# A state scan's C products: every C row spread to SBUF by DMA, VectorE multiplying pairs of states

## The chip, the cores and the metric

One core of a Trainium2 chip runs the whole program. The metric is device time in microseconds (us) of one execution, the median of several.

## What is computed

Four layers work one after the other on an image tensor x of shape (2, 96, 48, 48). The change touches one stage of the first layer, the selective scan of a 2D state space block: E = 192 channels, N = 16 states, K = 4 scan directions, L = 2304 positions. In the notation of the kernel, for each channel, direction and state n, along the positions i:

```
h[n, i] = exp(-A[n] * dlt[i]) * h[n, i-1] + B[n, i] * v'[n, i]
y[i]    = sum over n of C[n, i] * h[n, i]        (+ Ds * x, further down)
```

B and C belong to an image and a state, not to a channel, so each of their rows is needed on all the partitions (channels) of its image. The four directions' y are added up. The other layers and stages are the same in both kernels.

## The kernel before

Two images of 192 channels make T = 3 tiles of 128 partitions. A tile's scan over one direction is cut into NSEG = 3 segments of SEG = 768 positions. One (tile, direction, segment) is a **unit** u; there are U = 36, each with N = 16 states, so J = 576 **steps** j. All of it is in `l0_scan`, with the order of every engine written out by hand and counted semaphores between them. For step j:

- SyncE (`loads`, lines 696 to 700) brings a unit's dlt, na, B rows (Bp), v and C rows (Cp). B and C rows lie there in bf16 in three parts that sum to f32.
- TensorE spreads the B row of state n over the 128 partitions into PSUM: `b_rows`, two matmuls by a selecting matrix (line 729).
- ScalarE writes r = tanh(...) (line 889) and the decay exp(-A dlt) into PSUM (line 879, in two parts).
- VectorE makes r = (r + 1) * B, `b_r` (line 804, four steps ahead: AHEAD = 4).
- GpSimd multiplies two states of r by v, `times_v` (line 842, 1536 elements per partition). All of GpSimd's operands are in SBUF.
- VectorE runs the recurrence, `tensor_tensor_scan` (line 830), with the decay from PSUM and r from SBUF, into h.
- C times h is made in one of two ways. `BY_VECTOR` lists the states that VectorE multiplies: five in sixteen on average, 180 of the 576, one at a time (`times_c`, line 811), with C spread by TensorE into PSUM (`c_rows`, again line 729, from Cp). The other 396 are multiplied by GpSimd in 198 pairs (`times_c`, line 851), with C in SBUF: a DMA per image half reads two C rows from DRAM and writes them to 64 partitions each (line 712, tile `cb`, NCB = 4 slots).
- TensorE adds C*h into y in PSUM by an identity matmul, `add_y` (line 762), LATE = 5 steps behind.
- Once per unit, after state 9, VectorE makes the running sum of dlt for the next unit (`cumsum`, line 794). Once per unit ScalarE takes y out of PSUM (lines 872, 875).

What sets the order around the change: on VectorE a step is b_r(j+4), then times_c(j-1) where that state is VectorE's, then the scan of j. On GpSimd a pair of steps is times_v(j), then a pair of C products. PSUM holds one B row and one C row at a time, so a B row waits until the last one is used, and b_r and `c_rows` wait for each other too.

Of the kernel before, what the change touches and what calls it, by code (L numbers as in the profile page):

```python
# [592 lines left out]
def l0_scan(nc, a, ps, ident, Y, d):  # L593
# [5 lines left out]

    with ExitStack() as ctx:
        sb, sem = space(nc, ctx, "l0c")
        NR, NHV, NHP, NCB = 8, 3, 4, 4
        AHEAD, LATE, LAG = 4, 5, 6
        BY_VECTOR = ((2, 5, 10, 13), (2, 5, 8, 11, 12, 15))
        dlt, v, S = (sb(n, [128, 2, SEG]) for n in ("dlt", "v", "S"))
        Ds, dsum = sb("Ds", [128, T, K]), sb("dsum", [128, T])
        Bp, Cp = (sb(n, [3 * B * N, 2, SEG], BF16) for n in ("Bp", "Cp"))  # L610
# [13 lines left out]
        s_own, s_shared, s_tanh, s_w, s_b, s_c, s_S, s_init = map(  # L624
            sem, ("own", "shared", "tanh", "w", "b", "c", "S", "init"))
        PB, PC, PY = 0, SEG, 3 * BANK
# [5 lines left out]
        NLOAD = 5  # L632
# [4 lines left out]
        assert all(b == a + 1 and a // N == b // N for a, b in zip(others[::2], others[1::2]))  # L637

        def by_pool(j):
            return j not in with_c  # L640
# [4 lines left out]
        def pool_steps(j):  # L645
            return j - taken[j]
# [33 lines left out]

            return slice(BANK, SEG) if e % 2 == 0 else slice(0, MID)

        b_all, c_all, y_all = (ps[:, o:o + SEG] for o in (PB, PC, PY))
        da = [ps[:, o:o + SEG] for o in PDA]

        @block.sync
        def _(sp):
            def loads(u):
                t, k, c0 = place(u)
                i = u % 2  # L690
                if u >= 2:

                    sp.wait_ge(s_scan, (u - 1) * N + 1)
                if u % (K * NSEG) == 0:
                    sp.dma_start(sel[:, t % 2, :], a["sel"][t]).then_inc(s_sel[t % 2], 16)
                sp.dma_start(dlt[:, i, :], d["dlt"][t * K + k, :, c0:c0 + SEG]).then_inc(s_in[i], 16)
                sp.dma_start(na[:, i, :], d["na"][t * K + k]).then_inc(s_in[i], 16)
                sp.dma_start(Bp[:, i, :], d["bc"][k, 0, :, c0:c0 + SEG]).then_inc(s_in[i], 16)
                sp.dma_start(v[:, i, :], d["v"][t * K + k, :, c0:c0 + SEG]).then_inc(s_in[i], 16)
                sp.dma_start(Cp[:, i, :], d["bc"][k, 1, :, c0:c0 + SEG]).then_inc(s_in[i], 16)  # L700

            loads(0)
            sp.dma_start(Ds[:, :, :], a["Ds"]).then_inc(s_ds, 16)
            for j in range(J):
                u, n = divmod(j, N)
                if by_pool(j) and pool_steps(j) % 2 == 0:
                    t, k, c0 = place(u)
                    p = pool_steps(j)
                    if p >= NCB:
                        sp.wait_ge(s_hp, p - NCB + 2)  # L710
                    for i in range(2):
                        sp.dma_start(cb[64 * i:64 * i + 64, p % NCB:p % NCB + 2, :],
                                     d["cf"][k, 2 * t + i, n:n + 2, c0:c0 + SEG].unsqueeze(0)
                                     .to_broadcast([64, 2, SEG])).then_inc(s_cb[p % NCB // 2], 16)
                if n == (0 if u == 0 else 2) and u + 1 < U:
                    loads(u + 1)
            for i in range(2):
                sp.wait_ge(s_in[i], 16 * NLOAD * U // 2)
                sp.wait_ge(s_sel[i], 16 * ((T + 1 - i) // 2))
            for i in range(NCB // 2):  # L720
                sp.wait_ge(s_cb[i], 32 * len(range(2 * i, pool_steps(J), NCB)))

        @block.tensor
        def _(pe):
            def spread(rows, at, j, done):
                i, n = (j // N) % 2, j % N
                t = j // (N * NSEG * K)
                for lo, hi in pieces(at):
                    mm = pe.matmul(ps[:, lo:hi], sel[:, t % 2, n * 128:(n + 1) * 128], rows[:, i, lo - at:hi - at],  # L729
                                   start=True, stop=True)  # L730
                mm.then_inc(done, 1)

            def b_rows(j):
                u = j // N
                if j % N == 0:
                    pe.wait_ge(s_in[u % 2], (u // 2 + 1) * (16 * NLOAD))
                    t = u // (K * NSEG)
                    pe.wait_ge(s_sel[t % 2], 16 * (t // 2 + 1))
                if j:
                    pe.wait_ge(s_ub, j)  # L740
                if j - AHEAD - 1 > 0:
                    pe.wait_ge(s_hv, dve_steps(j - AHEAD - 1))
                spread(Bp, PB, j, s_b)

            def c_rows(j):
                if j:
                    pe.wait_ge(s_hv, dve_steps(j))
                pe.wait_ge(s_ub, min(j + AHEAD + 1, J))
                spread(Cp, PC, j, s_c)

            def add_y(j):
# [12 lines left out]
                mm.then_inc(s_y, 1)
                if place(u)[1] and 4 <= n < 4 + len(y_pieces(u)):
                    lo, hi, src = y_pieces(u)[n - 4]
                    pe.matmul(ps[:, lo:hi], ident[:, :], src, start=False, stop=False)

            for j in range(AHEAD + 1):
                b_rows(j)  # L770
            for j in range(J + LATE):
                if j < J and not by_pool(j):
                    c_rows(j)
                if j + AHEAD + 1 < J:
                    b_rows(j + AHEAD + 1)
                if j >= LATE:
                    add_y(j - LATE)

        @block.vector
        def _(dve):  # L780
# [36 lines left out]
            for j in range(J):  # L817
# [1702 lines left out]
```

## Time and profile before

| | |
|---|---|
| median of 3 runs | 2978.03 us |
| lowest, highest | 2972.81, 2978.46 us |
| the profiled execution: its own time | 2974.61 us |
| its span in the trace | 2972.7 us |
| its mean granted TensorE clock | 0.941 |

The profile is of one execution. Times are us unless marked ns; PE is TensorE, PEld its weight loads, DVE VectorE, ACT ScalarE, POOL GpSimd, SP SyncE. A row of the page names the line, the engine, the operation, what it writes and reads with shapes, the count, the busy time and mean length in ns, and the idle time before it with what ended that. The state scan runs from about 300 to 2001 us of the span.

### The profile page before, as it was taken

To read this page: it belongs to the slowest core of one execution; us is meant where nothing else is said; L and a number is where in the kernel's file an instruction comes from. 1 tells how busy PE (TensorE), PEld (TensorE's weight loads), DVE (VectorE), ACT (ScalarE), POOL (GpSimd) and SP (SyncE) were. 2 spreads that over 40 slices of the span, in tenths; PEclk is the share of its full clock that TensorE was granted. 3 is DMA by queue.
4 is the path that set the end of the run, shared out by engine and by line. 5 is a ranking of instruction groups with operands and counts; after the bars stand their busy time and mean duration, and the time that the engine had idled before them with its cause. 6 is when DMAs were issued, how large, how long until landed. Compare 5 with 4: busy or idle time off the path is not lost. (4 is left out here: it accounts for less than half of the span.)

```text
span 2972.7 us, 24549 instructions
## 1 busy us (share of the span) xinstructions
PE 2162.6 (73%) x7460; PEld 1057.5 (36%) x7460; DVE 2552.8 (86%) x2138; ACT 1575.5 (53%) x2301; POOL 1939.5 (65%) x645
## 2 busy tenths in 40 slices
PE   6853566676766666776666677678985999798579
PEld 3421223333332333333323333334432555354444
DVE  5678899999999999999999999986887777699620
ACT  1565677777777777777776777753230000362220
POOL 0165899999999999999999999984000000297000
PEclk9977799999999999999999999998897999899689
DMA  1276444444454444445444454535005443100360
GB/s 48 88 221 235 119 111 115 111 125 121 107 129 110 120 117 114 119 108 129 109 118 123 112 125 100 125 84 180 0 1 153 115 116 96 38 8 16 78 88 24
DMA packets 140258, 308.71 MB, mean 104 GB/s; under 512 B 47643, under 2 KB 63264, under 8 KB 135136
## 3 DMA queue, kind: packets, MB, share of 16 engines
q1 hardware_dynamic: 139040, 303.01, 40.3%
q10 hardware_dynamic: 1088, 4.13, 0.6%
q8 instruction: 62, 1.02, 0.2%
q14 instruction: 68, 0.56, 0.1%
HBM read 220.30 MB, written 46.87 MB: 90 GB/s over the span
## 5 line engine op out<-in xcount | busy, mean ns | idle before, releaser
L842 POOL TENSOR_TENSOR l0c_r<-l0c_r,l0c_v 128x1536 f32<-128x1536 f32 x288 | 990.6, 3447 | 51.1 <-DVE l0c_r L804 49.3
L879 ACT ACTIVATE ps<-l0c_dlt,l0c_na 128x512 f32<-128x512 f32 (+1 forms) x1152 | 626.1, 575 | 474.6 <-DVE l0c_h L830 460.1
L830 DVE TENSOR_TENSOR_SCAN l0c_h<-ps,l0c_h,l0c_r 128x768 f32<-128x768 f32 x384 | 693.3, 1806 | 1.2 <-issue 0.6
L851 POOL TENSOR_TENSOR l0c_hcp<-l0c_cb,l0c_h 128x1536 f32<-128x1536 f32 x198 | 682.9, 3449 | 1.4 <-issue 1.4
L762 PE MATMUL ps<-l0c_hcp,net_ident 128*128 128x512 f32 (+1 forms) x1584 | 586.6, 493 | 17.6 <-ACT l_Z L872 7.1
L889 ACT ACTIVATE l0c_r<-l0c_S,l0c_floor,l0c_na 128x768 f32<-128x768 f32 x576 | 580.1, 1014 | 18.0 <-issue 18.0
L729 PE MATMUL ps<-l0c_Bp,l0c_sel 96*128 96x512 bf16 (+1 forms) x1152 | 289.3, 333 | 379.5 <-DVE l0c_r L804 180.3
L804 DVE SCALAR_TENSOR_TENSOR l0c_r<-l0c_r,ps 128x768 f32<-128x768 f32 x576 | 533.1, 926 | 6.6 <-PE ps L729 3.9
L762 PEld LDWEIGHTS ps<-l0c_hcp,net_ident 128*128 128x128 f32 x1584 | 272.1, 192 | 268.7 <-issue 195.7
L830 DVE TENSOR_TENSOR_SCAN l0c_h<-ps,l0c_r 128x768 f32<-128x768 f32 x192 | 335.0, 1745 | 0.0
L1541 PE MATMUL ps<-l_prod,l_wa 128*96 128x384 f32 (+1 forms) x888 | 291.8, 492 | 25.8 <-DVE l_prod L1458 25.8
L729 PEld LDWEIGHTS ps<-l0c_Bp,l0c_sel 96*128 96x128 bf16 x1152 | 83.2, 97 | 571.5 <-DVE l0c_r L804 487.4
L762 PE MATMUL ps<-l0c_hcv,net_ident 128*128 128x512 f32 x720 | 266.0, 492 | 0.0
L167 POOL MEMSET l2g_pad<- 96x224 f32 (+1 forms) x8 | 1.8, 268 | 326.5 <-SPq L118 326.5
L1541 PEld LDWEIGHTS ps<-l_prod,l_wa 128*96 128x96 f32 (+1 forms) x888 | 146.3, 165 | 170.7 <-issue 161.6
L729 PE MATMUL ps<-l0c_Cp,l0c_sel 96*128 96x256 bf16 x360 | 88.9, 328 | 158.9 <-DVE l0c_r L804 138.4
L1678 PE MATMUL ps<-l_rows,l_diag 128*128 128x384 f32 x468 | 159.4, 503 | 16.1 <-DMA l_rows<-l2g_pad 11.3
L811 DVE TENSOR_TENSOR l0c_hcv<-ps,l0c_h 128x768 f32<-128x768 f32 x180 | 170.6, 948 | 0.1
L762 PEld LDWEIGHTS ps<-l0c_hcv,net_ident 128*128 128x128 f32 x720 | 123.9, 192 | 109.9 <-issue 88.9
L1607 POOL TENSOR_TENSOR l_accp<-l_accp,l_prod 128x1152 f32<-128x1152 f32 x54 | 142.3, 2636 | 29.2 <-ACT l_prod L1626 21.9
L1458 DVE TENSOR_TENSOR l_prod<-l_turned,l_other 128x2304 f32<-128x2304 f32 (+1 forms) x48 | 122.6, 2557 | 41.1 <-PE ps L1541 38.2
L1658 DVE SCALAR_TENSOR_TENSOR ps<-l_rows,net_kern,ps 128x1152 f32<-128x1152 f32 x105 | 149.4, 1423 | 3.7
(273 smaller groups left out, 2286.2 us busy)
## 6 DMA issues: line engine op xcount, KB each, us to landing
l0c_cb<-cf SPq DMA_DIRECT2D x396, 384.0 KB, 5.5
l_other<-l_p SPq DMA_DIRECT2D x22, 864.0 KB, 5.9
dlt<-l0s_dl SPq DMA_DIRECT2D x36, 384.0 KB, 2.3
v<-l0s_vv SPq DMA_DIRECT2D x36, 384.0 KB, 2.9
l0c_dlt<-dlt SPq DMA_DIRECT2D x36, 384.0 KB, 3.4
l0c_v<-v SPq DMA_DIRECT2D x36, 384.0 KB, 4.5
l_other<-l_p SPq DMA_DIRECT2D x22, 288.0 KB, 6.7
l0c_Bp<-bc SPq DMA_DIRECT2D x36, 144.0 KB, 3.7
```

The costliest lines, as they stand in the source:

```text
L729: mm = pe.matmul(ps[:, lo:hi], sel[:, t % 2, n * 128:(n + 1) * 128], rows[:, i, lo - at:hi - at], start=True, stop=True)
L762: mm = pe.matmul(ps[:, lo:hi], ident[:, :], hc[:, lo - PY:hi - PY], start=(n == 0), stop=(n == N - 1))
L804: dve.scalar_tensor_tensor(rj, rj, 1.0, b_all, ALU.add, ALU.mult).then_inc(s_ub, 1)
L811: dve.tensor_tensor(hcv[:, dve_steps(j) % NHV, :], c_all, h[:, j % N, :], ALU.mult).then_inc(s_hv, 1)
L830: dve.tensor_tensor_scan(h[:, n, :], da[j % 2], r[:, j % NR, :], init, ALU.mult, ALU.add).then_inc(s_scan, 1)
L842: pool.tensor_tensor(two, two, v[:, (j // N) % 2, :].unsqueeze(1).to_broadcast([128, 2, SEG]), ALU.mult).then_inc(s_w, 2)
L851: pool.tensor_tensor(hcp[:, p % NHP:p % NHP + 2, :], cb[:, p % NCB:p % NCB + 2, :], h[:, e % N:e % N + 2, :], ALU.mult).then_inc(s_hp, 2)
L879: act.activation(da[e % 2][:, part], dlt[:, i, part], ACT.Exp, scale=na[:, i, n:n + 1]).then_inc(done, 1)
L889: act.activation(r[:, j % NR, :], S[:, i, :], ACT.Tanh, bias=floor[:, :], scale=na[:, i, N + n:N + n + 1]).then_inc(s_tanh, 1)
L1541: mm = pe.matmul(ps[0:C, o:o + CH], wa[0:height, i, :], prod[0:height, n % NPR, c * CH:(c + 1) * CH], start=(i == 0), stop=(i == PT - 1))
L1658: ins = dve.scalar_tensor_tensor(sums, src, kern[:, tl, tap:tap + 1], sums, ALU.mult, ALU.add)
L1678: mm = pe.matmul(ps[:, o:o + CH], diag[:, tl, i, :], rows[:, tl, dy + 8 * c:dy + 8 * c + 8, dx:dx + W], start=(i == 0), stop=(i == NPE - 1))
```

## The change

- Every state's C rows come to SBUF by the spreading DMA, for VectorE's states too: 576 transfers in place of 396, into `cb` with NCB = 6 slots (three pairs). The slot is now given by the step's number j. SyncE waits for the engine that used the slot: GpSimd's or VectorE's count.
- `c_rows`, the tile Cp and its load, the PSUM area of C and the semaphore s_c are gone.
- VectorE's states are pairs now: (4, 5), (12, 13) in an even unit, (2, 3), (8, 9), (14, 15) in an odd one, 180 of 576 as before. `times_c` multiplies two states of h by two rows of cb in one instruction of 1536 elements, at the even step two steps later, with hcv at NHV = 4 slots.
- Waits that go: b_r's on s_c, and the B rows' on s_hv. `add_y` of a VectorE state waits until both of its pair are made.

```diff
-        NR, NHV, NHP, NCB = 8, 3, 4, 4
+        NR, NHV, NHP, NCB = 8, 4, 4, 6
-        BY_VECTOR = ((2, 5, 10, 13), (2, 5, 8, 11, 12, 15))
+        BY_VECTOR = ((4, 5, 12, 13), (2, 3, 8, 9, 14, 15))
...
-                sp.dma_start(Cp[:, i, :], d["bc"][k, 1, :, c0:c0 + SEG]).then_inc(s_in[i], 16)
...
-                if by_pool(j) and pool_steps(j) % 2 == 0:
+                if j % 2 == 0:
                     t, k, c0 = place(u)
-                    p = pool_steps(j)
-                    if p >= NCB:
-                        sp.wait_ge(s_hp, p - NCB + 2)
+                    if j >= NCB:
+
+                        if by_pool(j - NCB):
+                            sp.wait_ge(s_hp, pool_steps(j - NCB) + 2)
+                        else:
+                            sp.wait_ge(s_hv, dve_steps(j - NCB) + 2)
                     for i in range(2):
-                        sp.dma_start(cb[64 * i:64 * i + 64, p % NCB:p % NCB + 2, :],
+                        sp.dma_start(cb[64 * i:64 * i + 64, j % NCB:j % NCB + 2, :],
...
-                if j - AHEAD - 1 > 0:
-                    pe.wait_ge(s_hv, dve_steps(j - AHEAD - 1))
                 spread(Bp, PB, j, s_b)
-
-            def c_rows(j):
-                if j:
-                    pe.wait_ge(s_hv, dve_steps(j))
-                pe.wait_ge(s_ub, min(j + AHEAD + 1, J))
-                spread(Cp, PC, j, s_c)
...
-                    pe.wait_ge(s_hv, dve_steps(j) + 1)
+                    pe.wait_ge(s_hv, dve_steps(j) // 2 * 2 + 2)
...
-                if j > AHEAD:
-                    dve.wait_ge(s_c, dve_steps(j - AHEAD))
...
-            def times_c(j):
-                dve.wait_ge(s_scan, j + 1)
-                dve.wait_ge(s_c, dve_steps(j) + 1)
-                if dve_steps(j) >= NHV:
-                    dve.wait_ge(s_y, with_c[dve_steps(j) - NHV] + 1)
-                dve.tensor_tensor(hcv[:, dve_steps(j) % NHV, :], c_all, h[:, j % N, :], ALU.mult).then_inc(s_hv, 1)
+            def times_c(e):
+                q = dve_steps(e)
+                dve.wait_ge(s_scan, e + 2)
+                dve.wait_ge(s_cb[e % NCB // 2], 32 * (e // NCB + 1))
+                if q >= NHV:
+                    dve.wait_ge(s_y, with_c[q - NHV + 1] + 1)
+                dve.tensor_tensor(hcv[:, q % NHV:q % NHV + 2, :], cb[:, e % NCB:e % NCB + 2, :],
+                                  h[:, e % N:e % N + 2, :], ALU.mult).then_inc(s_hv, 2)
...
-                if j and not by_pool(j - 1):
-                    times_c(j - 1)
+                if j >= 2 and j % 2 == 0 and not by_pool(j - 2):
+                    times_c(j - 2)
...
-                for e in (j - 5, j - 4):
-                    if 0 <= e and e + 1 < J and by_pool(e) and pool_steps(e) % 2 == 0:
-                        times_c(e)
+                e = j - 4
+                if 0 <= e < J and by_pool(e):
+                    times_c(e)
```

VectorE's order inside the scan. Line 804 of before is 793 of the change (b_r), 830 is 821 (the scan), 811 is 801 (the C product). Before:

```order
L804 SCALAR_TENSOR_TENSOR l0c_r<-l0c_r,ps 128x768 [waits l0c_c,l0c_b,l0c_tanh]
L811 TENSOR_TENSOR l0c_hcv<-ps,l0c_h 128x768 [waits l0c_y,l0c_c,l0c_scan]
L830 SCALAR_TENSOR_TENSOR l0c_h<-ps,l0c_h,l0c_r 128x768 [waits l0c_w,l0c_shared,l0c_own]
L804 SCALAR_TENSOR_TENSOR l0c_r<-l0c_r,ps 128x768 [waits l0c_c,l0c_b,l0c_tanh]
L811 TENSOR_TENSOR l0c_hcv<-ps,l0c_h 128x768 [waits l0c_y,l0c_c,l0c_scan]
L830 SCALAR_TENSOR_TENSOR l0c_h<-ps,l0c_h,l0c_r 128x768 [waits l0c_w,l0c_shared,l0c_own]
```

With the change:

```order
L793 SCALAR_TENSOR_TENSOR l0c_r<-l0c_r,ps 128x768 [waits l0c_b,l0c_tanh]
L801 TENSOR_TENSOR l0c_hcv<-l0c_cb,l0c_h 128x1536 [waits l0c_cb0,l0c_y,l0c_scan]
L821 SCALAR_TENSOR_TENSOR l0c_h<-ps,l0c_h,l0c_r 128x768 [waits l0c_w,l0c_shared,l0c_own]
L793 SCALAR_TENSOR_TENSOR l0c_r<-l0c_r,ps 128x768 [waits l0c_b,l0c_tanh]
L821 SCALAR_TENSOR_TENSOR l0c_h<-ps,l0c_h,l0c_r 128x768 [waits l0c_w,l0c_shared,l0c_own]
```

One product of twice the length stands where two stood, it reads cb in place of PSUM, and it waits for the transfer (l0c_cb) in place of TensorE's row (l0c_c).

GpSimd's order with the change (833 is times_v, 842 times_c; before they were 842 and 851):

```order
L842 TENSOR_TENSOR l0c_hcp<-l0c_cb,l0c_h 128x1536 [waits l0c_cb1,l0c_y,l0c_scan]
L833 TENSOR_TENSOR l0c_r<-l0c_r,l0c_v 128x1536 [waits l0c_ub] x2
L842 TENSOR_TENSOR l0c_hcp<-l0c_cb,l0c_h 128x1536 [waits l0c_cb0,l0c_y,l0c_scan]
L833 TENSOR_TENSOR l0c_r<-l0c_r,l0c_v 128x1536 [waits l0c_ub]
L842 TENSOR_TENSOR l0c_hcp<-l0c_cb,l0c_h 128x1536 [waits l0c_cb1,l0c_y,l0c_scan]
```

The same products in the same numbers as before, 288 and 198; where VectorE has the pair, two v products follow one another.

## Rows read from the trace of the kernel before

**Rows 1.** The page: busy time, share of the span, instructions.
```profile
PE 2162.6 (73%) x7460; PEld 1057.5 (36%) x7460; DVE 2552.8 (86%) x2138; ACT 1575.5 (53%) x2301; POOL 1939.5 (65%) x645
```

**Rows 2.** Windows, inside the scan: us, busy (x) of PE, PEld, DVE, ACT, POOL, PEclk, DMA, GB/s.
```profile
406.00:1900.00 1494.00, 1032.83 (x3542) 473.83 (x3542) 1493.81 (x1212) 1073.66 (x1563) 1466.65 (x432) 0.99 0.48 117
```

**Rows 3.** The page, costliest groups: what the scan runs.
```profile
L842 POOL TENSOR_TENSOR l0c_r<-l0c_r,l0c_v 128x1536 f32<-128x1536 f32 x288 | 990.6, 3447 | 51.1 <-DVE l0c_r L804 49.3
L851 POOL TENSOR_TENSOR l0c_hcp<-l0c_cb,l0c_h 128x1536 f32<-128x1536 f32 x198 | 682.9, 3449 | 1.4 <-issue 1.4
L811 DVE TENSOR_TENSOR l0c_hcv<-ps,l0c_h 128x768 f32<-128x768 f32 x180 | 170.6, 948 | 0.1
L729 PE MATMUL ps<-l0c_Cp,l0c_sel 96*128 96x256 bf16 x360 | 88.9, 328 | 158.9 <-DVE l0c_r L804 138.4
```

**Rows 4.** Line 794, the running sum, once per unit: count, first and last start.
```profile
L794 DVE TENSOR_TENSOR_SCAN l0c_S<-l0c_dlt,l0c_S,ps x24: 1782/1784/1789, 339.2 to 1932.6; 128x768 f32<-128x768 f32 x24
```

**Rows 5.** Timeline of VectorE, 1250 to 1262 us (start us, us, engine, line).
```profile
1254.38 0.92 DVE L804 SCALAR_TENSOR_TENSOR l0c_r<-l0c_r,ps 128x768 f32<-128x768 f32 x1
1255.22 1.80 DVE L830 TENSOR_TENSOR_SCAN l0c_h<-ps,l0c_h,l0c_r 128x768 f32<-128x768 f32 x1
1256.95 0.92 DVE L804 SCALAR_TENSOR_TENSOR l0c_r<-l0c_r,ps 128x768 f32<-128x768 f32 x1
1257.80 0.94 DVE L811 TENSOR_TENSOR l0c_hcv<-ps,l0c_h 128x768 f32<-128x768 f32 x1
1258.66 1.80 DVE L830 TENSOR_TENSOR_SCAN l0c_h<-ps,l0c_h,l0c_r 128x768 f32<-128x768 f32 x1
```

**Rows 6.** Timeline of GpSimd, 1250 to 1262 us.
```profile
1250.26 3.45 POOL L851 TENSOR_TENSOR l0c_hcp<-l0c_cb,l0c_h 128x1536 f32<-128x1536 f32 x1
1253.66 3.45 POOL L842 TENSOR_TENSOR l0c_r<-l0c_r,l0c_v 128x1536 f32<-128x1536 f32 x1
1257.07 3.45 POOL L851 TENSOR_TENSOR l0c_hcp<-l0c_cb,l0c_h 128x1536 f32<-128x1536 f32 x1
```

**Rows 7.** Waits of 400 to 1900 us: GpSimd's own.
```profile
POOL l0c_r L842 <- DVE l0c_r L804: 27.4, 28, 1.8
```

**Rows 8.** Line 851: duration ns min/median/max.
```profile
L851 POOL TENSOR_TENSOR l0c_hcp<-l0c_cb,l0c_h x198: 3421/3444/3545, 319.1 to 1993.0; 128x1536 f32<-128x1536 f32 x198
```

**Rows 9.** Timeline, 2036.8 to 2042.5 us, the stage after the scan.
```profile
2037.10 1.20 POOL L1082 TENSOR_TENSOR l0n_wa<-l0n_wa,l0n_ma 128x480 f32<-128x480 f32 x1 [2.49 <-DMA l0n_mb<-in_mb]
2037.89 0.82 DVE L1068 TENSOR_TENSOR l0n_yk<-l0n_root,l0n_iv 128x384 f32<-128x384 f32 x1
...
2038.26 1.53 POOL L1083 TENSOR_TENSOR l0n_wb<-l0n_wb,l0n_mb 128x480 f32<-128x480 f32 x1
...
2039.57 1.44 DVE L1074 TENSOR_TENSOR l_Y<-l0n_yk,l_Y 128x1152 f32<-128x1152 f32 x1
2039.87 2.20 POOL L1085 TENSOR_TENSOR l0n_wa<-l0n_wa,l0n_wb 128x480 f32<-128x480 f32 x1
```

**Rows 10.** Lines 1068 and 1074, all of them: duration ns min/median/max.
```profile
L1068 DVE TENSOR_TENSOR l0n_yk<-l0n_root,l0n_iv x6: 495/660/937, 2030.2 to 2062.1; 128x384 f32<-128x384 f32 x6
L1074 DVE TENSOR_TENSOR l_Y<-l0n_yk,l_Y x6: 1341/1355/1436, 2039.6 to 2065.1; 128x1152 f32<-128x1152 f32 x6
```

**Rows 11.** The same stage, VectorE alone, GpSimd idle.
```profile
2063.88 2.61 DVE L1074 TENSOR_TENSOR l_Y<-l0n_yk,l_Y 128x1152 f32<-128x1152 f32 x2
```

**Rows 12.** Line 543 in the stage ahead: duration ns min/median/max.
```profile
L543 DVE TENSOR_SCALAR l0s_u<-l0s_e x18: 549/1159/3655, 126.9 to 281.3; 128x768 f32<-128x768 f32 x18
```

**Rows 13.** Timeline, 200 to 206 us, the stage ahead.
```profile
200.54 4.57 POOL L566 TENSOR_TENSOR l0s_parts<-l0s_rest,l0s_parts 128x2304 bf16<-128x2304 f32 x1
...
202.79 2.74 DVE L543 TENSOR_SCALAR l0s_u<-l0s_e 128x768 f32<-128x768 f32 x1
```

**Rows 14.** DMA of 400 to 1900 us: queue's share, issues.
```profile
q1 hardware_dynamic: 71895, 174.33, 47.5%
l0c_cb<-cf SPq DMA_DIRECT2D x352, 384.0 KB, 5.5
```

More of the change, by code:

```diff
@@ L604, in l0_scan @@
         sb, sem = space(nc, ctx, "l0c")
-        NR, NHV, NHP, NCB = 8, 3, 4, 4
+        NR, NHV, NHP, NCB = 8, 4, 4, 6
         AHEAD, LATE, LAG = 4, 5, 6
-        BY_VECTOR = ((2, 5, 10, 13), (2, 5, 8, 11, 12, 15))
+        BY_VECTOR = ((4, 5, 12, 13), (2, 3, 8, 9, 14, 15))
         dlt, v, S = (sb(n, [128, 2, SEG]) for n in ("dlt", "v", "S"))
         Ds, dsum = sb("Ds", [128, T, K]), sb("dsum", [128, T])
-        Bp, Cp = (sb(n, [3 * B * N, 2, SEG], BF16) for n in ("Bp", "Cp"))
+        Bp = sb("Bp", [3 * B * N, 2, SEG], BF16)
         sel = sb("sel", [3 * B * N, 2, N * 128], BF16)
@@ L623, in l0_scan @@
         s_ds, s_dsum = sem("ds"), sem("dsum")
-        s_own, s_shared, s_tanh, s_w, s_b, s_c, s_S, s_init = map(
-            sem, ("own", "shared", "tanh", "w", "b", "c", "S", "init"))
-        PB, PC, PY = 0, SEG, 3 * BANK
+        s_own, s_shared, s_tanh, s_w, s_b, s_S, s_init = map(
+            sem, ("own", "shared", "tanh", "w", "b", "S", "init"))
+        PB, PY = 0, 3 * BANK
         PDA = (5 * BANK, 8 * BANK - SEG)
@@ L631, in l0_scan @@
         J = U * N
-        NLOAD = 5
+        NLOAD = 4
         with_c = [u * N + n for u in range(U) for n in BY_VECTOR[u % len(BY_VECTOR)]]
@@ L636, in l0_scan @@
         taken = [sum(i < j for i in with_c) for j in range(J + 1)]
-        assert all(b == a + 1 and a // N == b // N for a, b in zip(others[::2], others[1::2]))
+        assert all(e + 1 in with_c for e in with_c if e % 2 == 0)
         def by_pool(j):
@@ L681, in shared_part @@
             return slice(BANK, SEG) if e % 2 == 0 else slice(0, MID)
-        b_all, c_all, y_all = (ps[:, o:o + SEG] for o in (PB, PC, PY))
+        b_all, y_all = (ps[:, o:o + SEG] for o in (PB, PY))
         da = [ps[:, o:o + SEG] for o in PDA]
@@ L705, in _ @@
                 u, n = divmod(j, N)
-                if by_pool(j) and pool_steps(j) % 2 == 0:
+                if j % 2 == 0:
                     t, k, c0 = place(u)
-                    p = pool_steps(j)
-                    if p >= NCB:
-                        sp.wait_ge(s_hp, p - NCB + 2)
+                    if j >= NCB:
[3 more added lines that the diff above has]
+                            sp.wait_ge(s_hv, dve_steps(j - NCB) + 2)
                     for i in range(2):
-                        sp.dma_start(cb[64 * i:64 * i + 64, p % NCB:p % NCB + 2, :],
+                        sp.dma_start(cb[64 * i:64 * i + 64, j % NCB:j % NCB + 2, :],
                                      d["cf"][k, 2 * t + i, n:n + 2, c0:c0 + SEG].unsqueeze(0)
-                                     .to_broadcast([64, 2, SEG])).then_inc(s_cb[p % NCB // 2], 16)
+                                     .to_broadcast([64, 2, SEG])).then_inc(s_cb[j % NCB // 2], 16)
                 if n == (0 if u == 0 else 2) and u + 1 < U:
@@ L720, in _ @@
             for i in range(NCB // 2):
-                sp.wait_ge(s_cb[i], 32 * len(range(2 * i, pool_steps(J), NCB)))
+                sp.wait_ge(s_cb[i], 32 * len(range(2 * i, J, NCB)))
         @block.tensor
@@ L771, in _ @@
             for j in range(J + LATE):
-                if j < J and not by_pool(j):
-                    c_rows(j)
                 if j + AHEAD + 1 < J:
@@ L831, in _ @@
                                        ).then_inc(s_scan, 1)
-            if not by_pool(J - 1):
-                times_c(J - 1)
+            if not by_pool(J - 2):
+                times_c(J - 2)
         @block.gpsimd
@@ L847, in times_c @@
                 pool.wait_ge(s_scan, e + 2)
-                pool.wait_ge(s_cb[p % NCB // 2], 32 * (p // NCB + 1))
+                pool.wait_ge(s_cb[e % NCB // 2], 32 * (e // NCB + 1))
                 if p >= NHP:
                     pool.wait_ge(s_y, others[p - NHP + 1] + 1)
-                pool.tensor_tensor(hcp[:, p % NHP:p % NHP + 2, :], cb[:, p % NCB:p % NCB + 2, :],
+                pool.tensor_tensor(hcp[:, p % NHP:p % NHP + 2, :], cb[:, e % NCB:e % NCB + 2, :],
                                    h[:, e % N:e % N + 2, :], ALU.mult).then_inc(s_hp, 2)
```

## The prediction, made before the changed kernel ran

> **What bounds the kernel now.** The page's first part puts VectorE ahead with 86% of the span, GpSimd at 65% [rows 1]. That is a mean over many stages, so the next view is the table of windows over the state scan, the only stage touched: in 1494.0 us VectorE is busy 1493.8 and GpSimd 1466.7, while TensorE and ScalarE have about 30% of their time free [rows 2]. VectorE is the bound and GpSimd is 98% full right behind it. GpSimd's idle time there comes from waiting for VectorE's b_r, 27.4 us in all [rows 7].
>
> VectorE's timeline shows no gap, so I count from start to start: b_r 0.84 us, scan 1.73, C multiplication of one state 0.86 [rows 5]. Two units (32 states, ten C multiplications, two running sums of about 1.70, which is 1.78 less the 0.08 by which neighbours overlap) come to 32 x 2.57 + 10 x 0.86 + 2 x 1.70 = 94.2 us. Measured: the running sums of units 1 and 35 start at 339.2 and 1932.6 [rows 4], 34 units apart, so **93.7 us for two units** (the scans without a carried start are a little shorter). GpSimd has 16 v products and 11 pairs of C products in two units, each 3.40 from start to start [rows 6]: 27 x 3.40 = **91.8 us**. There are 18 such double units.
>
> **TensorE, PSUM, SyncE.** The 360 matmuls that spread C, 88.9 us [rows 3], go. TensorE has 30% of its time free in the scan [rows 2] and what it owes VectorE, the B rows, comes while VectorE runs its 1.73 us scan: 0 us gained. The waits of b_r on C rows and of the B rows on the multiplication go with them, and VectorE had no gap for them to cause. In their place add_y of a VectorE pair waits for both states. That product runs two states later and add_y five states later, so 0.
>
> The C transfers grow from 396 to 576, and 36 loads of Cp go. 1494 us had 352 of them at a DMA share of 47.5%, 174 MB [rows 14]. In the same time there would be 160 more (63 MB) and 32 Cp less (5 MB), so about 63%, below full. A slot of cb is free again when the pair three pairs back is multiplied. The tightest is the pair (12, 13) of an even unit: in the count of boundaries below, GpSimd frees its slot at 11.8 and VectorE wants it at 23.9, so 12 us; all others have 17. Landing takes 5.5 us [rows 14] and the second transfer's issue about 0.6. SyncE's wait for a slot stands ahead of the next unit's loads, which are wanted eight states later. So 0, with that margin as the cover; once it is used up, each us of delay costs up to 90 us.
>
> **VectorE's own work.** No row has 1536 elements with both inputs in SBUF. The nearest is line 1074, 1152 elements: 1355 ns long [rows 10], and 2.61 - 1.36 = 1.25 us from start to start [rows 11]. From 768 elements to 1152 the length goes from 948 [rows 3] to 1355, 0.41 us for 384, so a pair takes 1.76 us, **1.65 from start to start**. It replaces 2 x 0.86. Gain 0.07 a pair, 90 pairs: 6 us. Two units come to 93.7 - 8.6 + 5 x 1.65 = **93.3 us** for VectorE, if nothing else happens.
>
> A rule of the Trainium skill ("VectorE: DVE Perf Modes", the section on the TRN2 errata) makes the fixed part 120 cycles with a PSUM source and 58 with SBUF; by that the pair would save (2 x 888 - 1594) / 0.96 = 190 ns and the change 17 us, an estimate. The trace doesn't bear it out: the 1152-element row has 155 ns over its 1.2 us of elements, the PSUM form 148.
>
> **The new cost: two SBUF inputs beside a busy GpSimd.** Every VectorE instruction of the scan reads one input from PSUM, and GpSimd's length hardly varies, 3421 to 3545 ns [rows 8]. After the change the multiplication reads cb and h, both SBUF. The stage behind the scan shows what that does [rows 9]. Line 1068 (two SBUF inputs) needs 0.495 us at best [rows 10]. At 2037.89 it starts beside a GpSimd product that ends at 2038.30, and it ends at 2038.71, 0.41 after it: it stood still. The next GpSimd product, 1.20 otherwise, takes 1.53. Then line 1074 starts first, at 2039.57, and the GpSimd product takes 2.20: it ends 1.06 after line 1074. One waits for the other, whichever came second. The stage ahead of the scan shows the same with a one-input form: 549 ns at best, 3655 at worst [rows 12], at 202.79 held until the 4.57 us product of GpSimd ended [rows 13]. In each of these rows VectorE gets in at the first boundary between two GpSimd instructions.
>
> The rule behind it is in the Trainium skill ("SBUF — State Buffer", section "Who interferes with whom"): a VectorE instruction with two SBUF inputs and a GpSimd instruction that reads SBUF exclude each other for their whole length. It speaks for every size; the rows reach 1152 elements.
>
> Price on GpSimd: held while a pair runs. The 0.495 us instruction cost it 0.33, so 1.76 costs about 1.76 - 0.17 = 1.59, with both ends between 1.5 and 1.76. Two units: 91.8 + 5 x 1.59 = **99.7 us**. GpSimd is now the bound, by 6.0 us over 93.7, at the least.
>
> Price on VectorE: w, the wait for the running GpSimd instruction, between 0 and 3.4 each; 93.3 + 5w. Random arrival has w = 1.7, so 101.8. The two are coupled, so I follow them from one pair to the next, time 0 being when a pair is let in. GpSimd's boundaries are at 1.59 + 3.40 = 4.99 and then every 3.40: 8.4, 11.8, 15.2, 18.6, 22.0, 25.4. VectorE comes with the next pair, after six states, at 1.65 + 6 x 2.57 = 17.1: let in at 18.6, w = 1.5. That is five GpSimd instructions, exactly its work for six states, so the pattern holds itself and VectorE's wait costs nothing on top. The one interval of eight states (it holds a running sum): 1.65 + 20.56 + 1.70 = 23.9, let in at 25.4, again GpSimd's own pace. The interval of six states with a running sum: 18.8, just past 18.6, so 22.0. GpSimd has then run ahead, its next v product must wait for a b_r (4.2 instead of 1.6), and the next interval is 17.8. Sum of the five: 18.6 + 25.4 + 18.6 + 22.0 + 17.8 = **102.4**. Where the scans are the shorter ones (one unit in three) 18.8 becomes 18.4 and the sum is 99.7. Mean of two thirds and one third: **101.4, or 7.7 more than 93.7**.
>
> **Sum.** 18 x 7.7 = 139 us. At the end the last pair stands between the last scan and its add_y: 1.65 for 0.86, about 1 us. The profiled execution took 2974.6, the median of the runs is 2978.0, 3.4 above. 2974.6 + 140 = **3115 us**. Other stages are not touched.
>
> **Rivals.**
> *GpSimd's pace alone* (the running sum never misses its boundary): 18 x 6.0 = 108, 3083. For it: the miss is by 0.2 us. It is inside my forecast's own range, 3075 to 3150. Together 0.78.
> *Longer waits.* VectorE isn't let in at the first boundary when GpSimd's next instruction is already queued, or arrives each time just behind one: w = 3.4, 93.3 + 17.0 = 110.3, 18 x 16.6 = 299, 3274. Against it: the first boundary sufficed in all rows read. 0.12, spread over 3150 to 3274.
> *No exclusion here, the other side.* If it needs something that the later stage has and this pair has not (other tiles, a start behind GpSimd), only the 6 us are left: 2968; by the 190 ns of the page it would be 2957. It decides if GpSimd's products stay at 3.45 us beside the pairs; the change turns slower only once a pair loses more than the 0.07 us that it saves. Against it: rows 9, 10 and 13. 0.07.
> *The C transfers come late.* At a share of 63% landing grows; beyond 12 us the even pairs wait, one us costs 18 to 90 us, so 3130 to 3250. For it: the share. Against it: the margin of twice the landing time. 0.03.
>
> **How the numbers follow.** The likeliest case is 3115. The range 3075 to 3160 takes in the bounds of GpSimd's loss (1.5 to 1.76 a pair, -8 to +15 us), both ends of the boundary question, and the near end of the longer waits; about 2 in 10 are left out. 0.2% is 6 us, what a measurement of this kernel can tell from none. Slower 0.93, from the three other cases; no exclusion gives 2968 or less, on the border: faster 0.05, same 0.02.
>
> **What would show it.** VectorE's C product has 90 instructions whose length, waiting included, has a mean near 3.4 us (1.76 and a mean wait of 1.7) with a shortest about 1.76. Of GpSimd's products some 90 are 5.0 us long, mostly v products, so their mean goes from 3.45 to about 3.9. GpSimd is busy over 97% of the scan; the running sums of units 1 and 35 are 1724 us apart where they were 1593. Wrong if GpSimd's longest stays near 3.5, if VectorE waits for cb, or if the C products average above 4.5.

## The result and the profile after

| | before | changed |
|---|---|---|
| median | 2975.4 us (4 runs) | 3127.8 us (4 runs, 3126.2 to 3132.8) |
| ratio | 1 | 1.0515, 95% interval 1.0496 to 1.0533 |
| span in the trace | 2972.7 | 3131.0 |
| the scan, start of the first running sum to start of the last y evacuation | 300 to 2001 | 298 to 2158 |

Slower by 5.15%, or 152 us, where 3115 was forecast. The profiled execution is the slowest of the four, 3132.8. All of it is in the scan: 1701 us became 1860, and what follows takes 973 for 971.

The page of the changed kernel, span and busy times (to be held against [rows 1]), then the table of windows for 406 to 1900 us (against [rows 2]; same columns):

```profile
span 3131.0 us, 23131 instructions
PE 2253.3 (72%) x7100; PEld 1098.5 (35%) x7100; DVE 2694.7 (86%) x2048; ACT 1573.3 (50%) x2301; POOL 2044.1 (65%) x645
```

```profile
406.00:1900.00 1494.00, 1015.05 (x2936) 464.65 (x2935) 1481.61 (x1036) 978.74 (x1429) 1424.96 (x395) 0.88 0.60 143
```

VectorE is as busy as ever by this view, 1481.6 of 1494 us, and GpSimd less than before, 1425 for 1467. Both numbers mislead. VectorE's busy time now contains standing still, which the lengths show. The costliest groups (against [rows 3]), then the lengths in ns as min/median/max and the running sums (against [rows 8] and [rows 4]):

```profile
L833 POOL TENSOR_TENSOR l0c_r<-l0c_r,l0c_v 128x1536 f32<-128x1536 f32 x288 | 1091.8, 3800 | 105.4 <-DVE l0c_r L793 105.4
L842 POOL TENSOR_TENSOR l0c_hcp<-l0c_cb,l0c_h 128x1536 f32<-128x1536 f32 x198 | 682.0, 3445 | 0.0
L793 DVE SCALAR_TENSOR_TENSOR l0c_r<-l0c_r,ps 128x768 f32<-128x768 f32 x576 | 533.1, 925 | 23.3 <-PE ps L730 19.9
L801 DVE TENSOR_TENSOR l0c_hcv<-l0c_cb,l0c_h 128x1536 f32<-128x1536 f32 x90 | 298.8, 3320 | 0.1
```

```profile
L801 DVE TENSOR_TENSOR l0c_hcv<-l0c_cb,l0c_h x90: 1757/3162/6593, 326.0 to 2151.3; 128x1536 f32<-128x1536 f32 x90
L833 POOL TENSOR_TENSOR l0c_r<-l0c_r,l0c_v x288: 3418/3442/4971, 305.3 to 2140.4; 128x1536 f32<-128x1536 f32 x144
L842 POOL TENSOR_TENSOR l0c_hcp<-l0c_cb,l0c_h x198: 3425/3442/3471, 317.0 to 2147.2; 128x1536 f32<-128x1536 f32 x198
L785 DVE TENSOR_TENSOR_SCAN l0c_S<-l0c_dlt,l0c_S,ps x24: 1778/1784/1815, 338.0 to 2084.2; 128x768 f32<-128x768 f32 x24
```

The 90 pair products take 3320 ns on average where the shortest takes 1757: 141 us of VectorE's busy time are waits inside the instruction. GpSimd's v products (line 833) went from 3447 to 3800 on average and to 4971 at the longest, while its C products (842) stayed at 3445. The running sums of units 1 and 35 lie 1746.2 us apart, 1593.4 before, so two units take **102.7 us for 93.7**.

GpSimd's timeline with VectorE's pair products, 1233 to 1261 us (start, length, engine, line):

```profile
1233.29 2.56 DVE L801 TENSOR_TENSOR l0c_hcv<-l0c_cb,l0c_h 128x1536 f32<-128x1536 f32 x1
1234.19 8.34 POOL L833 TENSOR_TENSOR l0c_r<-l0c_r,l0c_v 128x1536 f32<-128x1536 f32 x2
...
1242.48 3.45 POOL L842 TENSOR_TENSOR l0c_hcp<-l0c_cb,l0c_h 128x1536 f32<-128x1536 f32 x1
1245.89 3.44 POOL L833 TENSOR_TENSOR l0c_r<-l0c_r,l0c_v 128x1536 f32<-128x1536 f32 x1
1249.28 3.45 POOL L842 TENSOR_TENSOR l0c_hcp<-l0c_cb,l0c_h 128x1536 f32<-128x1536 f32 x1
1250.85 3.50 DVE L801 TENSOR_TENSOR l0c_hcv<-l0c_cb,l0c_h 128x1536 f32<-128x1536 f32 x1
1252.68 8.35 POOL L833 TENSOR_TENSOR l0c_r<-l0c_r,l0c_v 128x1536 f32<-128x1536 f32 x2
```

VectorE's product starts at 1233.29 beside a GpSimd instruction that ends at 1234.2, and ends at 1235.85, 1.6 us after that. The row of GpSimd's two v products is 8.34 long, 1.5 more than two of them [rows 6]. The next pair starts at 1250.85, GpSimd's C product ends at 1252.7, the pair ends at 1254.35: 18.50 us after the last one, which is five GpSimd products and one hold of 1.51. I wrote down the ends of all 90 pair products. Their 89 distances repeat in this order, from one pair of units to the next (the very last one is 15.8):

```
measured                                            forecast
25.3                (17 times, 28.7 once)           25.4
18.5                (33 times with the last row)    18.6
21.9                (17 times)                      22.0
18.0                (18 times, 21.4 twice)          17.8
18.5                                                18.6
```

The third interval, with the running sum in it, is 21.9 in every pair of units up to the last. Its parts in unit 15, one of the units with the shorter scans (rows of all engines, 1098 to 1116 us; in brackets the idle time before an instruction and what ended it):

```profile
1101.10 0.95 DVE L793 SCALAR_TENSOR_TENSOR l0c_r<-l0c_r,ps 128x768 f32<-128x768 f32 x1 [0.56 <-PE ps L730]
...
1107.29 3.45 POOL L842 TENSOR_TENSOR l0c_hcp<-l0c_cb,l0c_h 128x1536 f32<-128x1536 f32 x1
...
1110.69 3.44 POOL L833 TENSOR_TENSOR l0c_r<-l0c_r,l0c_v 128x1536 f32<-128x1536 f32 x1
1111.22 4.53 DVE L801 TENSOR_TENSOR l0c_hcv<-l0c_cb,l0c_h 128x1536 f32<-128x1536 f32 x1
```

VectorE stood 0.56 us for a late B row of TensorE, which the kernel before never made it do between 340 and 1930 us, and its pair product came 0.53 us after GpSimd's next instruction had started. In 17 of 17 such intervals VectorE stood for a B row, 0.14 to 1.23 us each time. In the six units with the shorter scans it would otherwise have come 0.03 to 0.08 us in front of GpSimd's next start. What that is worth stands under the count of boundaries below.

The DMA share and landing time of the C transfers, 400 to 2000 us (against [rows 14]), give no sign of a bottleneck, and VectorE has no wait for cb:

```profile
q1 hardware_dynamic: 88683, 225.82, 59.2%
l0c_cb<-cf SPq DMA_DIRECT2D x500, 384.0 KB, 5.5
```

### The profile page after: what moved, and what is told of

The parts are those of the page before. It is cut to its first block and busy times, and to the rows that moved or that the text cites. A ratio compares the mean times of both kernels' runs of the same rounds, so it can differ in the third digit from the quotient of the medians.

```text
span 3131.0 us, 23131 instructions
## 1 busy us (share of the span) xinstructions
PE 2253.3 (72%) x7100; PEld 1098.5 (35%) x7100; DVE 2694.7 (86%) x2048; ACT 1573.3 (50%) x2301; POOL 2044.1 (65%) x645
## 5 line engine op out<-in xcount | busy, mean ns | idle before, releaser
L833 POOL TENSOR_TENSOR l0c_r<-l0c_r,l0c_v 128x1536 f32<-128x1536 f32 x288 | 1091.8, 3800 | 105.4 <-DVE l0c_r L793 105.4
L730 PE MATMUL ps<-l0c_Bp,l0c_sel 96*128 96x512 bf16 (+1 forms) x1152 | 331.8, 375 | 595.2 <-DVE l0c_r L793 567.6
L755 PE MATMUL ps<-l0c_hcp,net_ident 128*128 128x512 f32 (+1 forms) x1584 | 725.5, 589 | 29.2 <-ACT l_Z L863 16.7
L755 PEld LDWEIGHTS ps<-l0c_hcp,net_ident 128*128 128x128 f32 x1584 | 333.9, 234 | 363.5 <-issue 288.5
L801 DVE TENSOR_TENSOR l0c_hcv<-l0c_cb,l0c_h 128x1536 f32<-128x1536 f32 x90 | 298.8, 3320 | 0.1
L1598 POOL TENSOR_TENSOR l_accp<-l_accp,l_prod 128x1152 f32<-128x1152 f32 x54 | 142.3, 2636 | 29.2 <-ACT l_prod L1617 21.9
L1669 PEld LDWEIGHTS ps<-l_rows,l_diag 128*128 128x128 f32 x468 | 90.9, 195 | 84.0 <-issue 11.5
```

The source lines that it names most:

```text
L801: dve.tensor_tensor(hcv[:, q % NHV:q % NHV + 2, :], cb[:, e % NCB:e % NCB + 2, :], h[:, e % N:e % N + 2, :], ALU.mult).then_inc(s_hv, 2)
L833: pool.tensor_tensor(two, two, v[:, (j // N) % 2, :].unsqueeze(1).to_broadcast([128, 2, SEG]), ALU.mult).then_inc(s_w, 2)
L1669: mm = pe.matmul(ps[:, o:o + CH], diag[:, tl, i, :], rows[:, tl, dy + 8 * c:dy + 8 * c + 8, dx:dx + W], start=(i == 0), stop=(i == NPE - 1))
```

## The experiments

The theory: a VectorE instruction with two SBUF inputs and a GpSimd instruction exclude each other. VectorE is let in at a boundary between two GpSimd instructions, so its waits come in steps of GpSimd's 3.40 us, and GpSimd loses 1.5 us for each. The rivals: the load of the C transfers; plain sums of work; TensorE's granted clock, which fell from 0.99 to 0.87 in the scan, something I hadn't foreseen.

### One input from PSUM

VectorE's 180 products take a constant, written to a free PSUM bank at the start, in place of C, so C is left out there.

```diff
-                dve.tensor_tensor(hcv[:, q % NHV:q % NHV + 2, :], cb[:, e % NCB:e % NCB + 2, :],
-                                  h[:, e % N:e % N + 2, :], ALU.mult).then_inc(s_hv, 2)
+                two = lambda x: x.rearrange("p a s -> p (a s)").rearrange("p (c n) -> p c n", n=BANK)
+                dve.tensor_tensor(two(hcv[:, q % NHV:q % NHV + 2, :]),
+                                  ps[:, 2 * BANK:3 * BANK].unsqueeze(1).to_broadcast([128, 3, BANK]),
+                                  two(h[:, e % N:e % N + 2, :]), ALU.mult).then_inc(s_hv, 2)
```

> VectorE's pair product reads a constant from PSUM in place of cb (C is left out of VectorE's 180 states); all 576 transfers, all waits and the pairing stay. Exclusion of two SBUF inputs against GpSimd: the 90 products last 1.75 to 1.85 us each, GpSimd's longest falls from 4.97 to under 3.6, and the time is that of before less the 6 us that pairing saves: 2969 (2962 to 2978). Rival, the load of the transfers (DMA share 59% for 47%): nothing changes, 3120 to 3130. Rival, TensorE's lower granted clock (0.87 for 0.98 in the scan) as the cause: the time stays high as far as the clock stays low.

Measured: 2980.6 us, ratio 1.0019 (1.0009 to 1.0028). Lengths of VectorE's pair product and of GpSimd's v product in this run:

```profile
L804 DVE TENSOR_TENSOR l0c_hcv<-ps,l0c_h x90: 1739/1740/1756, 327.3 to 2002.0; 128x1536 f32<-128x1536 f32 x90
...
L837 POOL TENSOR_TENSOR l0c_r<-l0c_r,l0c_v x288: 3417/3439/3500, 306.7 to 1990.6; 128x1536 f32<-128x1536 f32 x144
```

1739 to 1756 ns, no waiting, and GpSimd's longest is 3500. With all transfers, all pairing and all semaphores as in the change, **147 of the 152 us are gone** by moving one operand of 90 instructions out of SBUF. The transfers as the cause fall with it, and so does TensorE's clock as the main one: it stood at 0.93 here (table further down), half of its fall, with nearly all of the time given back. C is left out in this run, so it is a test and not a way out. The Trainium skill ("SBUF — State Buffer", section "Who interferes with whom") says that a VectorE instruction with two SBUF inputs and a GpSimd instruction reading SBUF shut each other out; the run agrees, GpSimd's longest being 3.50 us here and 4.97 in the change. But it is 11 us above what I expected, and over the end of my range, 2978; the section on TensorE's clock looks into that.

### The pair as two instructions

```diff
-                dve.tensor_tensor(hcv[:, q % NHV:q % NHV + 2, :], cb[:, e % NCB:e % NCB + 2, :],
-                                  h[:, e % N:e % N + 2, :], ALU.mult).then_inc(s_hv, 2)
+                for i in range(2):
+                    dve.tensor_tensor(hcv[:, q % NHV + i, :], cb[:, e % NCB + i, :],
+                                      h[:, e % N + i, :], ALU.mult).then_inc(s_hv, 1)
```

> The pair product as two instructions of 768 elements, both inputs in SBUF as in the change. If the two engines take turns at each boundary, the GpSimd product that waits gets in between the two halves and the second half waits for all of it: 3.4 us more for each of 90 pairs on VectorE, which then needs 20.4 us for six states where GpSimd needs 18.6; about 114 us for two units in place of 102.7, 3330 us in all (3250 to 3420). If VectorE keeps what it holds for its next instruction, only a second fixed part is added: 3128 to 3135.

Measured: 3322.7 us, ratio 1.117 (1.1147 to 1.1192). The lengths of the 180 halves, then one pair in the timeline:

```profile
L802 DVE TENSOR_TENSOR l0c_hcv<-l0c_cb,l0c_h x180: 943/2124/4176, 327.8 to 2344.4; 128x768 f32<-128x768 f32 x180
```

```profile
1209.98 3.44 POOL L843 TENSOR_TENSOR l0c_hcp<-l0c_cb,l0c_h 128x1536 f32<-128x1536 f32 x1
...
1212.31 6.02 DVE L802 TENSOR_TENSOR l0c_hcv<-l0c_cb,l0c_h 128x768 f32<-128x768 f32 x2
1213.38 4.12 POOL L834 TENSOR_TENSOR l0c_r<-l0c_r,l0c_v 128x1536 f32<-128x1536 f32 x1
```

The first half waits until 1213.4, when GpSimd's product ends. The second half waits for the whole next product of GpSimd (1213.38 to 1217.50, held 0.7 us by the first half) and ends at 1218.3. Here the engines take turns at each boundary, and nothing is kept for the next instruction; the time, 7 us under the 3330 expected of that, fits it. The same work in two pieces costs 195 us more.

### Cutting running sums: in the long interval, in the short one, and in the kernel before

```diff
+                if u >= 2 and u % 2 == 1:
+                    dve.tensor_tensor_scan(S[:, i, SEG - 1:SEG], dlt[:, i, SEG - 1:SEG], b_all[:, 0:1], init,
+                                           ALU.add, ALU.bypass).then_inc(s_S, 1)
+                    return
```

The sums of odd units run in the interval of eight states (above), those of even units (`u % 2 == 0`) in one of six. Each variant takes 17 x 1.65 = 28 us of work from VectorE, and S is wrong in those units. The third is the kernel before with the sums of odd units cut.

> The change, with 17 of 36 running sums (odd units) cut to one element, so S is wrong there: 1.65 us of VectorE work less, in the interval of eight states, where VectorE then waits for GpSimd's boundary anyway. Boundaries: nothing, 3128 (3120 to 3132). Rival, VectorE's work counts as a sum: 17 x 1.65 = 28 less, 3100.

> The change, with 17 other running sums (even units from 2) cut to one element: the same 1.65 us of VectorE work less, but in an interval of six states, which then ends at GpSimd's fifth boundary and not its sixth. Boundaries: 21.9 + 18.0 become 18.5 + 18.5, 2.9 us less for two units, 49 less in all, and the three extra misses seen (3.4 each) may go too: 3075 (3065 to 3085). Rival, a sum of VectorE's work: 28 less, 3100. Rival, GpSimd's pace alone is the bound: nothing, 3128.

> The kernel before with the same 17 running sums (odd units) cut to one element as in the run on the change that moved the time by 3 us only. VectorE's work counts as a sum here: 17 x 1.65 = 28 less, 2948, unless GpSimd (91.8 of 93.7 us for two units) takes over: then no less than 2955 or so. So 2945 to 2958.

Measured:

```
                                  median     against the same kernel with all sums
change, sums of odd units cut     3125.0     -2.8   (ratio to before 1.0506, 1.0491 to 1.0522)
change, sums of even units cut    3088.8     -39.0  (ratio to before 1.0388, 1.0365 to 1.0412)
before, sums of odd units cut     2955.3     -19.0  (ratio 0.9937, 0.9922 to 0.9952)
```

The same 28 us of VectorE's work are worth 3 (no more than the runs vary), 39 or 19. No sum of work gives that; boundaries do. In the second run the ends are 18.5 apart where 21.9 and 18.0 stood. It missed my 3065 to 3085 by 4 us: in the profiled execution (3100.2, the slowest of the four) one pair was a boundary late in four places and the next one too (21.9, 21.4, 18.0 for 55.5, 5.8 us each). In all eight of these intervals VectorE had stood 0.8 to 1.4 us for a late B row, and its pairs came between 0.01 us in front of GpSimd's next start and 0.14 us behind it. In the kernel before, GpSimd takes over before the 28 are reached. Its waits for VectorE, 340 to 1930 us, fell from 28.6 to 8.9 us, and VectorE now waits for it:

```profile
POOL l0c_r L846 <- DVE l0c_r L808: 8.9, 11, 2.2
DVE l0c_h L834 <- POOL l0c_r L846: 2.6, 6, 0.7
```

### Four pairs in two units, in the change and before

```diff
-        BY_VECTOR = ((4, 5, 12, 13), (2, 3, 8, 9, 14, 15))
+        BY_VECTOR = ((4, 5, 12, 13),)
```

> The change with two pairs in every unit on VectorE, (4, 5) and (12, 13), so four in 32 states for five; GpSimd, the bound, gets one product more (28 for 27). Boundaries: every interval is one of eight states and seven GpSimd instructions, 4 x 25.4 = 101.6 us for two units where the change measures 102.7, so about 20 us faster although the bound engine has more work: 3108 (3100 to 3118). Rival, the sum of GpSimd's work alone: 18 x (3.4 - 1.6) = 32 more, 3160.

> The kernel before with VectorE taking eight states in 32 for ten, the counterpart of the run above where nothing excludes anything: GpSimd has 28 products, 95.2 us for two units, and becomes the bound over VectorE's 92.0: 18 x 1.5 = 27 slower, 3003 (2995 to 3010). If GpSimd's 3.40 from start to start could be beaten when it never waits, less.

Measured: on the change 3121.8 us (ratio 1.0496, 1.0480 to 1.0512), 6 less than the change, which is not clear of noise (the two intervals overlap) and is outside my 3100 to 3118; the bare sum for GpSimd had said 32 more, and that is refuted. On the kernel before, with its list cut to (2, 5, 10, 13), 3002.8 (1.0095, 1.0078 to 1.0112), 29 more than the 2974.2 measured beside it, where the sum says 27. The pair lengths and running sums of the first:

```profile
L801 DVE TENSOR_TENSOR l0c_hcv<-l0c_cb,l0c_h x72: 1749/3352/8372, 329.6 to 2133.4; 128x1536 f32<-128x1536 f32 x72
...
L785 DVE TENSOR_TENSOR_SCAN l0c_S<-l0c_dlt,l0c_S,ps x24: 1781/1789/1790, 341.6 to 2071.7; 128x768 f32<-128x768 f32 x24
```

Two units take (2071.7 - 341.6) / 17 = 101.8 us, 101.6 expected. The work of one GpSimd product more costs nothing, but the 20 us that I expected to gain are not there. Nine pairs came 21.8 us after the last one was let in, just in front of a boundary that the forecast had put out of reach, and were let in there (1749 to 1762 ns). VectorE was then ahead, stood about 1.8 us for GpSimd's v product, and its next pair came at 25.3 to 25.6, in six of the nine cases too late for the boundary there, so that this interval took 28.7. And three pairs waited past a whole further GpSimd product (up to 8372 ns); I can't explain when that happens. It is in the change too, once in 90:

```profile
760.75 3.47 POOL L842 TENSOR_TENSOR l0c_hcp<-l0c_cb,l0c_h 128x1536 f32<-128x1536 f32 x1
...
762.62 6.59 DVE L801 TENSOR_TENSOR l0c_hcv<-l0c_cb,l0c_h 128x1536 f32<-128x1536 f32 x1
...
764.16 3.44 POOL L833 TENSOR_TENSOR l0c_r<-l0c_r,l0c_v 128x1536 f32<-128x1536 f32 x1
```

GpSimd's product ends at 764.2, but the next one starts there and VectorE gets in at 767.6.

### TensorE's clock

Two runs with spare matmuls. On the change, into a PSUM bank that nobody reads:

```diff
+            def idle_rows(j):
+                i, n, t = (j // N) % 2, j % N, j // (N * NSEG * K)
+                for w in (BANK, SEG - BANK):
+                    pe.matmul(ps[:, 2 * BANK:2 * BANK + w], sel[:, t % 2, n * 128:(n + 1) * 128], Bp[:, i, 0:w],
+                              start=True, stop=True)
...
+                if j < J and not by_pool(j):
+                    idle_rows(j)
```

> The change with the removed 360 matmuls put back as spare work: they spread a B row into an unused PSUM bank, nobody reads it, no wait. If TensorE's fall to a granted 0.87 in the scan comes from its having less to do, the clock returns to 0.95 or more, VectorE's waits for B rows (20 us in all, none to speak of before) vanish and with them some of the missed boundaries: 3105 to 3120. If TensorE isn't on the path: 3125 to 3132. If more work only delays the B rows: 3130 to 3150.

On the run with one input from PSUM, the same matmuls just ahead of the B rows, into their place:

```diff
+                if not by_pool(j):
+                    i, n, t = (j // N) % 2, j % N, j // (N * NSEG * K)
+                    for lo, hi in pieces(PB):
+                        pe.matmul(ps[:, lo:hi], sel[:, t % 2, n * 128:(n + 1) * 128], Bp[:, i, lo:hi],
+                                  start=True, stop=True)
```

> The run with one input from PSUM (2980.6, 11 above what I had worked out) with 360 spare matmuls of a B row, into the same PSUM place just ahead of the real ones, at VectorE's 180 states. There TensorE's granted clock in the scan was 0.92 for 0.98 before and VectorE stood 9.5 us for B rows. If less work on TensorE lowered the clock and that cost the 11 us: clock 0.97 or more, waits for B rows under 2 us, 2968 to 2974. If the clock isn't about the amount of work: 0.90 to 0.93 and 2980 to 2990.

And the kernel before with the additional transfers alone (the spare tile, its semaphores and the waits on them are left out of the excerpt):

```diff
+                if not by_pool(j):
...
+                    for i in range(2):
+                        sp.dma_start(spare[64 * i:64 * i + 64, q % 4:q % 4 + 1, :],
+                                     d["cf"][k, 2 * t + i, n:n + 1, c0:c0 + SEG].unsqueeze(0)
+                                     .to_broadcast([64, 1, SEG])).then_inc(s_spare[q % 4], 16)
```

> The kernel before with the C rows of VectorE's 180 states also spread by DMA, 360 transfers of 192 KB into a spare tile that nobody reads, so as many bytes as in the change. If the load of the transfers costs nothing: 2972 to 2978, clock 0.98 in the scan. If it is what lowers TensorE's clock or delays anything: 2980 to 2990, as in the run with one input from PSUM.

Measured: 3130.9 (1.0527, 1.0511 to 1.0543), 2988.3 (1.0039, 1.0024 to 1.0054) and 2976.6 (0.9999, 0.9989 to 1.0009). The table of windows, 340 to 1930 us, of before, the change, one input from PSUM, and these three runs in that order; the third number from the end is the granted clock, then the DMA share:

```profile
340.00:1930.00 1590.00, 1096.96 (x3762) 502.88 (x3762) 1589.81 (x1290) 1142.04 (x1661) 1559.60 (x459) 0.99 0.48 117
```

```profile
340.00:1930.00 1590.00, 1082.15 (x3119) 495.11 (x3120) 1575.90 (x1102) 1042.11 (x1520) 1516.63 (x420) 0.87 0.60 142
```

```profile
340.00:1930.00 1590.00, 1119.13 (x3410) 506.70 (x3410) 1579.71 (x1200) 1135.40 (x1654) 1553.23 (x457) 0.93 0.65 155
```

```profile
340.00:1930.00 1590.00, 1121.85 (x3430) 523.89 (x3430) 1577.58 (x1101) 1041.34 (x1519) 1516.64 (x420) 0.88 0.59 142
```

```profile
340.00:1930.00 1590.00, 1167.04 (x3740) 538.08 (x3741) 1577.93 (x1199) 1135.36 (x1654) 1551.13 (x456) 0.93 0.65 155
```

```profile
340.00:1930.00 1590.00, 1107.30 (x3760) 508.12 (x3761) 1589.39 (x1290) 1141.42 (x1661) 1558.64 (x459) 0.98 0.67 159
```

The clock stayed at 0.88 and 0.93 with the matmuls back, so the missing matmuls are not what lowered it, and neither run got faster; the second got slower, by 7 or 8 us, hardly clear of noise. At a DMA share of 0.67 the kernel before keeps its clock (0.98) and its time. So the transfers are free here, and the fall of the clock isn't theirs. What the trace of the run with one PSUM input shows of the fall is TensorE around a y evacuation:

```profile
1213.44 0.50 PE L730 MATMUL ps<-l0c_Bp,l0c_sel 96*128 96x512 bf16 x2 [0.78 <-DVE l0c_r L795]
...
1217.68 0.50 PE L730 MATMUL ps<-l0c_Bp,l0c_sel 96*128 96x512 bf16 x2 [2.45 <-DVE l0c_r L795]
...
1219.36 2.93 PE L755 MATMUL ps<-l0c_hcp,net_ident 128*128 128x512 f32 x4 [1.17 <-ACT l_Z L867]
...
1222.08 0.79 PE L730 MATMUL ps<-l0c_Bp,l0c_sel 96*128 96x512 bf16 x2
...
1222.97 0.96 DVE L795 SCALAR_TENSOR_TENSOR l0c_r<-l0c_r,ps 128x768 f32<-128x768 f32 x1 [1.05 <-PE ps L730]
```

TensorE had stood 2.45 us behind the pair product (1.34 at most in the same place before), worked 0.5, and stood 1.17 for ScalarE. The four matmuls after that took 2.93 us; in the kernel before the same four behind the same evacuation took 1.56, so the level here is 1.2 GHz for 2.4. The next B row comes late and VectorE stands 1.05. That happened 13 times between 340 and 1930 us, 9.5 us, about the 11 that this run was over my figure. The longer standing of TensorE goes with the lower clock in every run (0.83 in the split one, with the most of it), but no run changed that alone, so it stays a reading.

Of these runs none that computes all of it beats the kernel before: VectorE's 93.7 us for two units stand there without a gap, and with C in SBUF the exclusion added 8 at the least (101.8, four pairs).

## Why the prediction was right, point by point

- **The bound and its margins** (93.7 us for two units, GpSimd at 91.8): right. The kernel before with eight states on VectorE in place of ten turned over to GpSimd as the sum said, 3002.8 for 3003.
- **TensorE's removed matmuls, 0 us**: right that nothing is gained, wrong that nothing is lost. The pair product makes TensorE stand longer, its clock fell to 0.87, and B rows came late, 12.9 us of waits in the change (340 to 1930 us). What these small waits cost is in the count below. In the run without exclusion they are 9.5 us, most of the 11 over my figure.
- **The transfers, 0 us**: right. Share 59% (63% worked out), landing 5.5 us, and no change when they are added to the kernel before.
- **VectorE's own gain, 6 us**: the shortest pair, 1757 ns, is what was taken (1.76). The gain itself is seen nowhere in a time, since the run that could show it lost more to the late B rows. The Trainium skill's 58 against 120 cycles ("VectorE: DVE Perf Modes", the section on the TRN2 errata) is not borne out: 1536 elements take 1740 ns with one PSUM input and 1757 with two SBUF inputs, the second is longer.
- **GpSimd's loss of 1.59 a pair**: 1.51 measured (18.51 less five times 3.40). Only 69 of 90 pairs cost it that ((3800 - 3442) x 288 / 1500); in most of the others it was waiting for a b_r anyway.
- **The count of boundaries**: 18.6, 25.4, 18.6, 22.0, 17.8 forecast, 18.5, 25.3, 18.5, 21.9, 18.0 measured. What failed is the one unit in three with shorter scans, which was to come at 18.4 and be let in at 18.6. It missed each time, so the sum is 102.2 everywhere and the mean not 101.4. That is 0.8 x 17 = 13 us of the 22 that the distance of the running sums is over the forecast (1746 for 1724); the three further misses (21.4 twice, 28.7 once) are the other 9.
- **Why the six units missed**: two steps of the forecast are behind it. GpSimd's loss was taken 0.08 too large, so the boundary was at 18.5. And B rows were taken to cost nothing: VectorE's own work brings it to 18.45 in these six units, and with the waits for B rows it came at 18.6 to 19.7. Without the waits the six would have come 0.03 to 0.08 us in front of GpSimd's next start. In the change and the runs on it with cut sums or four pairs, every pair that came 0.04 to 0.35 us in front was let in there, and of six that came within 0.03 one was; so four of the six would have made it, and two are open. Both intervals of 21.4 also hold 0.8 us of such waits and missed by 0.1 or less. So late B rows cost six to eight boundaries of 2.9 us, 17 to 23 of the 152, an estimate from these rows that no run tested by taking the waits away.
- **The signs**: GpSimd's products of 5.0 us are 69 where some 90 were named, and it is busy 95.4% of the window 406 to 1900 where over 97% was: in 17 places it stood 4.3 us for VectorE's b_r, 73 us in all, after a pair that had missed a boundary. The forecast counts that wait (4.2) in its 17.8 but not in this sign.
- **The rivals**: no exclusion is refuted by rows and run. GpSimd's pace alone (3083) is refuted too: cutting the even units' sums gave 39 us, which a pure GpSimd bound can't give. Longer waits than the first boundary exist, once in 90 in the change, so that rival had a part of its mechanism, at a price of 3 us.

## What to carry to other kernels

Before an operand moves from PSUM to SBUF, look at what GpSimd does beside it: here 90 VectorE instructions with two SBUF inputs, 158 us of work in all, cost 152 us because GpSimd was 98% busy. Where two engines exclude each other and one never pauses, count boundaries, not work: taking 28 us from VectorE gave 3 or 39 according to the place, giving the bound engine one product more cost nothing, and where a pair comes within a tenth of a us of a boundary, a small delay by a third engine decides. And read an instruction's mean length against its shortest; a wait of this kind is inside the busy time, so no view of waits shows it.

## What the hardware showed that was not expected

- A VectorE product that waits for GpSimd is nearly always let in at GpSimd's next boundary, but was passed over in rare cases (once in 90 in the change, with 6.59 us; three times in 72 with four pairs, up to 8.37). When it came within 0.03 us in front of GpSimd's next start it waited for all of that one in five cases of six.
- TensorE's granted clock in the scan went from 0.99 to 0.87 in the change and 0.93 with one PSUM input, at about the same share of busy time (69%, 68% and 70% of 1590 us, of fewer and longer matmuls), and 360 spare matmuls didn't bring it back. What lowers it is open.
- Raising the DMA share from 0.48 to 0.67 changed nothing: ratio 0.9999, within 0.1%.
